# Silu by one ScalarE instruction in a selective-scan kernel, and a reordered block end

## The chip, the cores and the metric

The kernel runs on one core of a Trainium2 chip. The metric is the device time of one execution in microseconds (us). Three runs of the kernel before gave a median of 3261.13 us (3260.6 to 3262.81).

## The reference, cut to what matters

Four sequences of 1024 tokens and 512 channels go through a conditioned block with two state-space scans, one forward in time and one backward, each over 1024 inner channels and 16 states.

```python
ada = jax.nn.silu(c) @ Wada.T + bada                  # shift, scale, gate
x_ssm = _ln(_ln(x) * (1 + scale) + shift)             # skip is the inner value
mz = x_ssm @ Wz.T + bz ;  mx = x_ssm @ Wx.T + bx
act_mx = jax.nn.silu(mx)                              # what the change is about
z1 = ssm(mz @ Wc1.T + bc1) ;  z2 = flip(ssm(flip(mz @ Wc2.T + bc2)))
# inside ssm: delta = softplus(dlt @ Wdt.T + bdt), h = exp(delta*A)*h + delta*B*u, y = sum_n h*C + u*D
out = (act_mx * z1 + act_mx * z2) @ Wf.T + bf + skip
return x + gate * out
```

## The kernel before, in words

A setup part (`setup_kernel`, some 230 us) normalises the tokens, folds weights and stores intermediates. The main part (`ssm_kernel`) is one straight program of 64 units. A unit k is one tile of 128 inner channels of one direction of one sequence, all 1024 tokens: of each 16 units the first eight are the forward tiles of a sequence, the next eight its backward tiles. A unit has 16 chunks c, one for each state. In this text a unit's chunk is written as scan 0, Exp 5 and so on. Five engines run their own instruction streams in program order and meet at semaphores; SyncE (SP) issues nearly all DMAs.

For each chunk: ScalarE (ACT) computes the decay exp(delta*A) (L1218) into `dec` or into a PSUM slot; the inflow delta*B*u is made in one of three ways, by the letter of the chunk in `KINDS = "EVAVEVAPAVAPAPAV"`: E by a TensorE (PE) product with a diagonal (L939), A by ScalarE's scaling (L1159) that PE transposes (L927), V and P by GpSimd's (POOL) product in `bst` (L1257). VectorE (DVE) scans (L1352). The product with C is VectorE's for V (L1361) and GpSimd's for the others (L1262). PE transposes and sums all 16 in `y` (L916), four chunks late.

Around the scans each unit prepares the next one in the PSUM pair `mb` (1024 columns, two halves): at chunk 3 PE's product for delta (`delta_product`, L876), at chunk 4 ScalarE's `copy_y` (L1150) and `softplus_start` (Abs L1115, Exp L1117), at chunk 5 `softplus_end` (Ln, L1121) and VectorE's `finish_delta` (L1283), from chunk 7 or 9 on PE's z product (L887), VectorE's `inflow_half` (L1293) and ScalarE's `skip_half` and `copy_dut`.

The gate silu(mx) is needed once for each tile of each sequence, 32 times. It is made in the units k with k%16 from 1 to 8 (`has_mx`); these are called mx units here. Their mx product runs on PE at chunks 13 to 15 and at chunk 0 of the next unit (`mx_part`, L897). ScalarE makes the sigmoid of each half with four functions (`sigmoid_half`: Relu L1134, Exp L1137, Ln L1139, Exp L1142), half 0 at chunk 15, half 1 at chunk 1 of the next unit; VectorE's `silu_half` (L1303) multiplies each by mx + bx. The result in `silu` is stored by SP at chunk 5 and loaded again for the backward tiles.

The units k with k%16 from 9 to 15 and 0 (but not k = 0) have `gate_y` at chunk 7 (L1315) and are called gate units. From the second sequence on, a block of the output projection goes with them: PE's `project` at chunk 15 and at chunk 0 of the next unit, and VectorE's `read_projection` (L1319, four instructions) at chunk 1. `delta_product` waits for the reader of `mb` from the unit before: `silu_ready` or `proj_read`.

The tables of ScalarE: line 243 of the setup part is `nc.scalar.preload_act_table_set("natural_log_exp_and_others")`, and no other line names a table set.

Of the kernel before, what the change touches and what calls it, by code (L numbers as in the profile page):

```python
# [27 lines left out]
def setup_kernel(nc, t, scratch):  # L28

    with ExitStack() as ctx:  # L30
# [288 lines left out]
        def _(dve):  # L319
# [62 lines left out]
            nc.vector.tensor_copy(dbias[:, 1:2], ps[6][0:RD, DT * RD:DT * RD + 1]).then_inc(proj_ready[1], 1)  # L382
            dve.wait_ge(proj_ready[1], 2)
            dve.wait_ge(bcz_ready, NF)
            nc.vector.tensor_scalar(par[:, 0, :, PBX], par[:, 0, :, PBX], -LOW, None, ALU.add).then_inc(par_ready, 1)
            nc.vector.tensor_tensor(par[:, :, :, PZD], par[:, :, :, PBZ], par[:, :, :, PDP],
                                    ALU.mult).then_inc(par_ready, 1)

# [157 lines left out]
def ssm_kernel(nc, t, scratch):  # L546

    with ExitStack() as ctx:
# [3 lines left out]
        def sem(name):  # L552
            return ctx.enter_context(nc.semaphore(name))
# [29 lines left out]
            "turned", "dut_mm", "scaled", "bt_ready", "dut_ready"))  # L583
        mx_mm, ytr_mm, ud_mm, summed, proj_mm = (sem(n) for n in (
            "mx_mm", "ytr_mm", "ud_mm", "summed", "proj_mm"))
        soft_step, soft_ready, ud_ready, decay_ready, y_read, sig_step, sig_ready = (sem(n) for n in (
            "soft_step", "soft_ready", "ud_ready", "decay_ready", "y_read", "sig_step", "sig_ready"))
        delta_ready, du_ready, scanned, dve_prod, silu_ready, gated, proj_read = (sem(n) for n in (
            "delta_ready", "du_ready", "scanned", "dve_prod", "silu_ready", "gated", "proj_read"))
        pool_b, pool_prod = (sem(n) for n in ("pool_b", "pool_prod"))  # L590
# [109 lines left out]
        def _(sp):  # L700
# [68 lines left out]
            for k in range(NU):  # L769
# [3 lines left out]
                for c in range(N):  # L773
# [52 lines left out]
                        sp.wait_ge(y_read, k)  # L826
                        sp.dma_start(scratch["yf"][pair(k - 1)], yrd[:]).then_inc(y_out, 16)
                    if c == 5 and k > 0 and has_mx(k - 1) and not backward(k - 1):
                        sp.wait_ge(silu_ready, 2 * mx_index(k - 1) + 2)
                        sp.dma_start(scratch["si"][pair(k - 1)], silu[:]).then_inc(si_out, 16)  # L830
                    if c == 6 and e == ET - 2 and k + 2 < NU:
                        sp.wait_ge(dps_mm, 2 * (k + 2))
# [30 lines left out]
        def _(pe):  # L863
            def delta_product(k):
                pe.wait_ge(wdt_in[k % 2], 16 * (k // 2 + 1))
                pe.wait_ge(dl_in, 48 * (k // ET + 1))
                for h in range(2):
                    if k >= 2 and has_mx(k - 2):
                        pe.wait_ge(silu_ready, 2 * mx_index(k - 2) + h + 1)
                    elif k >= 2 and dbc_job(k - 2) is not None:  # L870
                        pe.wait_ge(dbc_ready, 2 * dbc_job(k - 2) + h + 1)
                    elif k >= 2 and h == 0 and projection_of(k - 2) is not None:
                        pe.wait_ge(proj_read, projection_of(k - 2) + 1)
                    elif k >= 1:
                        pe.wait_ge(dut_ready, 2 * k - 1 + h)
                    nc.tensor.matmul(mb[h], wdt[:, k % 2, :], dl[:, half(h)], start=True, stop=True).then_inc(dps_mm, 1)  # L876
# [230 lines left out]
        def _(act):  # L1107

            def softplus_start(k):
                if k > 0:  # L1110
                    act.wait_ge(delta_ready, k)
                if k >= 2 and has_mx(k - 2):
                    act.wait_ge(silu_ready, 2 * mx_index(k - 2) + 2)
                act.wait_ge(dps_mm, 2 * k + 2)
                nc.scalar.activation(soft[:], mbw[:], ACT.Abs).then_inc(soft_step, 1)  # L1115
                act.wait_ge(soft_step, 2 * k + 1)
                nc.scalar.activation(soft[:], soft[:], ACT.Exp, scale=-1.0).then_inc(soft_step, 1)  # L1117
# [10 lines left out]
                nc.scalar.activation(ud[:, half(h)], z_bank(k, h), ACT.Identity, scale=par[:, f // ET, f % ET, PDP:PDP + 1],  # L1128
                                     bias=par[:, f // ET, f % ET, PZD:PZD + 1]).then_inc(ud_ready, 1)

            def sigmoid_half(k, h):
                i = 2 * mx_index(k) + h
                act.wait_ge(mx_mm, i + 1)
                nc.scalar.activation(soft[:, half(h)], mb[h], ACT.Relu,  # L1134
                                     bias=par[:, 0, k % ET, PBX:PBX + 1]).then_inc(sig_step, 1)
                act.wait_ge(sig_step, 3 * i + 1)
                nc.scalar.activation(soft[:, half(h)], soft[:, half(h)], ACT.Exp, scale=-1.0).then_inc(sig_step, 1)  # L1137
                act.wait_ge(sig_step, 3 * i + 2)
                nc.scalar.activation(soft[:, half(h)], soft[:, half(h)], ACT.Ln, scale=math.exp(-LOW),  # L1139
                                     bias=1.0).then_inc(sig_step, 1)  # L1140
                act.wait_ge(sig_step, 3 * i + 3)
                nc.scalar.activation(soft[:, half(h)], soft[:, half(h)], ACT.Exp, scale=-1.0).then_inc(sig_ready, 1)  # L1142

            def copy_y(k):
                act.wait_ge(summed, N * (k + 1))
# [55 lines left out]
            for k in range(NU):  # L1201
                f, zs = wtile(k), z_step(k)
                new_b = (k + 1) % ET == 0
                for c in range(N):
                    q = N * k + c
                    if c == 0:
                        act.wait_ge(delta_ready, k + 1)
                    if kind(q) in "AE":
                        if before("AE", q) > 0:
                            act.wait_ge(scanned, TURNED[before("AE", q) - 1] + 1)  # L1210
                        decays = dec[:]
                    else:
                        if q >= 2:
                            wait_scanned_out(act, q - 2)
                        elif q == 1:
                            act.wait_ge(bt_ready, 1)
                        decays = slot[q % 2][:]
                    nc.scalar.activation(decays, delta[:, k % 2, :], ACT.Exp,  # L1218
                                         scale=par[:, f // ET, f % ET, PA + c:PA + c + 1]).then_inc(decay_ready, 1)
                    if c == LAG and k > 0:  # L1220
                        copy_y(k - 1)
                    if c == 1 and k % ET == 0:
                        make_diagonal(k // ET, 1)
                    if c in SCALE_STEPS:
                        for n, h in SCALE_STEPS[c]:
                            scale_half(N * k + n, h)
                    if c == 1 and k > 0 and has_mx(k - 1):
                        sigmoid_half(k - 1, 1)
                    if c in (0, 1) and k > 0 and dbc_job(k - 1) is not None:
                        evict_dbc(dbc_job(k - 1), c)  # L1230
                    if k + 1 < NU:
                        if c == 4:
                            softplus_start(k + 1)
                        if c == 5:
                            softplus_end(k + 1)
                        if c in (zs + 2, zs + 4):
                            skip_half(k + 1, (c - zs - 2) // 2)
                        if c == zs + 4 and new_b:
                            copy_bt((k + 1) // ET)
                        if c == 14 and new_b:  # L1240
                            make_diagonal((k + 1) // ET, 0)
                        if c == zs + 5:
                            copy_dut(k + 1, 0)
                        if c == min(zs + 7, N - 1):
                            copy_dut(k + 1, 1)
                    if c == 15 and has_mx(k):
                        sigmoid_half(k, 0)
            copy_y(NU - 1)

        @block.gpsimd  # L1250
# [27 lines left out]
        def _(dve):  # L1278
# [15 lines left out]
                                               scalar=par[:, f // ET, f % ET, PBZ:PBZ + 1],  # L1294
                                               in1=delta[:, k % 2, half(h)], op0=ALU.add, op1=ALU.mult).then_inc(du_ready, 1)

            def silu_half(k, h):
                dve.wait_ge(sig_ready, 2 * mx_index(k) + h + 1)
                if h == 0:
                    stored = k // (2 * ET) * (ET - 1) + (ET - 1 if backward(k) else k % ET - 1)  # L1300
                    if stored > 0:
                        dve.wait_ge(si_out, 16 * stored)
                nc.vector.scalar_tensor_tensor(out=silu[:, half(h)], in0=mb[h],  # L1303
                                               scalar=par[:, 1, k % ET, PBX:PBX + 1],
                                               in1=soft[:, half(h)], op0=ALU.add, op1=ALU.mult).then_inc(silu_ready, 1)

            def gate_y(k):
                b, e = k // (2 * ET), k % ET
                if e > 0:
                    dve.wait_ge(si_in, 16 * ((ET - 1) * b + e))  # L1310
                else:
                    dve.wait_ge(silu_ready, 2 * mx_index(k) + 2)
                bank = mbw if k < NU - 1 else slot[0]
                dve.wait_ge(ytr_mm, 2 * pair(k) + 2)
                nc.vector.tensor_tensor(ybuf[:], bank[:], silu[:], ALU.mult).then_inc(gated, 1)  # L1315
# [21 lines left out]
            for k in range(NU):  # L1337
                zs = z_step(k)
                step = -1 if backward(k) else 1
                for c in range(N):  # L1340
# [8 lines left out]
                    if q >= HR:  # L1349
# [1 line left out]
                    h = slot[q % 2] if kind(q) == "V" else hbuf[:, q % HR, :]  # L1351
                    nc.vector.tensor_tensor_scan(h[:, ::step], decays[:, ::step], inflows[:, ::step], 0.0,  # L1352
                                                 ALU.mult, ALU.add).then_inc(scanned, 1)
                    if c == 1 and k > 0 and projection_of(k - 1) is not None:
                        read_projection(projection_of(k - 1), mb[0])
                    if c == 5 and k + 1 < NU:
                        finish_delta(k + 1)
                    if kind(q) == "V":
# [1 line left out]
                        dve.wait_ge(c_in[c], 16 * (q // SEQ + 1))  # L1360
                        nc.vector.tensor_tensor(hbuf[:, q % HR, :], slot[q % 2][:], cres[:, c, :],  # L1361
                                                ALU.mult).then_inc(dve_prod, 1)
                    if c == 1 and k > 0:
                        if has_mx(k - 1):
                            silu_half(k - 1, 1)
                    if c == 5 and k == NU - 1:
                        read_projection(projection_of(k), mb[1])
                    if c == 7 and gates(k):
                        gate_y(k - 1)
                    if c in (zs + 2, zs + 4) and k + 1 < NU:  # L1370
                        inflow_half(k + 1, (c - zs - 2) // 2)
                    if c == 15 and has_mx(k):
                        silu_half(k, 0)
            gate_y(NU - 1)
            dve.wait_ge(rest_in, 32 * ET)
            for i in range(TAIL, B * ET):
# [78 lines left out]
```

## Time and profile before

| what | value |
| --- | --- |
| median of 3 runs | 3261.13 us |
| profiled execution, its own time | 3260.72 us |
| its span, first to last instruction | 3258.9 us |
| mean granted TensorE clock | 0.987 |
| units 0 to 63, first scan to last scan | 234.1 to 3198.9 us |

All durations below are from this one profiled execution; 1.8 us of its time lie around its span. A timeline row reads: start in us, duration in us, engine, line, operation, output<-input, shapes, number of merged instructions, and in brackets the idle time of the engine before it with what ended it. Successive instructions of an engine overlap a little, so that a start can lie some 0.1 us before the end of the one before.

### The profile page before, as it was taken

What the parts mean: (1) busy time and instruction counts of PE and PEld (TensorE: products, weight loads), DVE (VectorE), ACT (ScalarE), POOL (GpSimd) and SP (SyncE); (2) the same over time, 40 slices, a digit from 0 to 9 for tenths busy, and PEclk for the clock granted to TensorE, in tenths of its full rate; (3) what the DMA queues carried; (4) which work ended last, traced back from release to release, by engine and by line L of the source; (5) the groups of instructions that cost most, each with busy time, mean ns of one, the idle gap of its engine ahead of it and who ended that gap; (6) DMA issues with size and microseconds to landing.
All of it is one profiled execution on the core that took longest, in us unless ns stands there. A gap on an engine that the chain in (4) does not pass through costs nothing.

```text
span 3258.9 us, 54891 instructions
## 1 busy us (share of the span) xinstructions
PE 2982.0 (92%) x19924; PEld 2368.9 (73%) x19924; DVE 3015.8 (93%) x2008; ACT 2676.7 (82%) x5150; POOL 2901.4 (89%) x1280
## 2 busy tenths in 40 slices
PE   8979999999999999999989999899999999899999
PEld 5866666666767667678877666678777666677789
DVE  2839999999999999999999999999999999999994
ACT  1548999988888999987788999987878999988772
POOL 0539999999999999999999999999999999999993
PEclk9989999999999999999999999999999999999999
DMA  5774334645474343644574334645566333645463
GB/s 223 276 241 176 127 131 141 211 164 175 159 279 161 127 134 132 221 153 147 167 263 169 131 121 135 224 140 167 167 218 215 118 134 131 227 141 166 154 201 109
DMA packets 207197, 560.40 MB, mean 172 GB/s; under 512 B 20216, under 2 KB 66744, under 8 KB 202704
## 3 DMA queue, kind: packets, MB, share of 16 engines
q1 hardware_dynamic: 203568, 538.01, 49.6%
q10 hardware_dynamic: 2208, 10.49, 0.9%
q0 software_dynamic: 1152, 8.39, 0.7%
q8 instruction: 159, 2.61, 0.3%
q14 instruction: 110, 0.90, 0.1%
HBM read 476.19 MB, written 80.63 MB: 171 GB/s over the span
## 4 chain that ended last, share of the span: by engine, by line
PE 50%; ACT 21%; DVE 12%; issue 10%; DVEq 0%; ACTq 0%
PE y L916 14%; PE slot L927 10%; PE mb L887 9%; ACT abuf L1159 8%; PE mb L1000 6%; DVE hbuf L1352 6%; ACT slot L1218 3%; DVE hbuf L1361 3%; PE mb L897 3%; PE slot L939 3%; DVE slot L1352 3%; ACT dec L1218 2%; ACT soft L1115 2%; PE mb L958 2%; PE mb L993 1%
## 5 line engine op out<-in xcount | busy, mean ns | idle before, releaser
L1262 POOL TENSOR_TENSOR hbuf<-hbuf,cres 128x1024 f32<-128x1024 f32 x704 | 1665.5, 2380 | 138.1 <-DVE hbuf L1352 137.9
L1257 POOL TENSOR_TENSOR bst<-bst,du 128x1024 f32<-128x1024 f32 x512 | 1224.6, 2392 | 33.5 <-DVE du L1293 33.5
L1352 DVE TENSOR_TENSOR_SCAN hbuf<-dec,slot 128x1024 f32<-128x1024 f32 x512 | 1165.0, 2275 | 35.6 <-PE slot L939 28.4
L916 PE MATMUL y<-ident,hbuf 128*128 128x128 f32 x8192 | 1016.2, 273 | 0.1
L916 PEld LDWEIGHTS y<-ident,hbuf 128*128 128x128 f32 x8192 | 924.2, 141 | 104.6 <-issue 104.0
L1159 ACT ACTIVATE abuf<-dut,bt 128x128 f32<-128x128 f32 x3072 | 964.7, 387 | 0.0
L1352 DVE TENSOR_TENSOR_SCAN slot<-slot,bst 128x1024 f32<-128x1024 f32 x320 | 728.2, 2276 | 21.1 <-ACT slot L1218 21.0
L1218 ACT ACTIVATE slot<-delta,par 128x1024 f32<-128x1024 f32 x512 | 568.2, 1110 | 196.4 <-DVE hbuf L1361 183.4
L1218 ACT ACTIVATE dec<-delta,par 128x1024 f32<-128x1024 f32 x512 | 584.1, 1141 | 113.8 <-DVE hbuf L1352 113.2
L927 PE MATMUL slot<-ident,abuf 128*128 128x128 f32 x3072 | 409.2, 276 | 168.2 <-ACT abuf L1159 157.4
L927 PEld LDWEIGHTS slot<-ident,abuf 128*128 128x128 f32 x3072 | 339.5, 141 | 301.0 <-ACT abuf L1159 240.2
L887 PE MATMUL mb<-xn,wzs 128*128 128x512 f32 x1008 | 478.9, 597 | 14.8 <-DVE ybuf L1315 11.7
L1352 DVE TENSOR_TENSOR_SCAN hbuf<-slot,bst 128x1024 f32<-128x1024 f32 x192 | 434.7, 2264 | 0.1
L1361 DVE TENSOR_TENSOR hbuf<-slot,cres 128x1024 f32<-128x1024 f32 x320 | 390.7, 1221 | 8.0
L939 PEld LDWEIGHTS slot<-diag,dut 128*128 128x128 f32 x2048 | 261.3, 203 | 103.8 <-issue 100.2
L939 PE MATMUL slot<-diag,dut 128*128 128x128 f32 x2048 | 270.2, 289 | 40.7 <-DVE hbuf L1352 37.7
L887 PEld LDWEIGHTS mb<-xn,wzs 128*128 128x128 f32 x1008 | 171.6, 190 | 145.8 <-issue 143.6
L897 PE MATMUL mb<-xn,wx 128*128 128x512 f32 x512 | 240.9, 593 | 0.0
L1000 PE MATMUL mb<-ybuf,wf 128*128 128x128 f32 x1504 | 176.4, 275 | 3.6 <-issue 3.6
L1000 PEld LDWEIGHTS mb<-ybuf,wf 128*128 128x128 f32 x1504 | 171.9, 192 | 4.0 <-issue 4.0
L876 PE MATMUL mb<-dl,wdt 81*128 81x512 f32 x252 | 130.9, 622 | 11.9 <-DVE silu L1303 10.0
L897 PEld LDWEIGHTS mb<-xn,wx 128*128 128x128 f32 x512 | 87.3, 190 | 61.2 <-issue 61.2
(170 smaller groups left out, 2283.9 us busy)
## 6 DMA issues: line engine op xcount, KB each, us to landing
bst<-bc_s SPq DMA_DIRECT2D x512, 512.0 KB, 4.0
cres<-bc_s SPq DMA_DIRECT2D x128, 512.0 KB, 7.0
wzs<-wz_s SPq DMA_DIRECT2D x64, 256.0 KB, 4.2
yf_s<-yrd SPq DMA_DIRECT2D x32, 512.0 KB, 5.4
ybuf<-yf_s SPq DMA_DIRECT2D x32, 512.0 KB, 5.0
yg_s<-ybuf SPq DMA_DIRECT2D x31, 512.0 KB, 4.4
si_s<-silu SPq DMA_DIRECT2D x28, 512.0 KB, 6.1
silu<-si_s SPq DMA_DIRECT2D x28, 512.0 KB, 5.4
```

Source lines behind the costliest of these rows:

```text
L887: last = nc.tensor.matmul(z_bank(k, h), wz[:, i * P:(i + 1) * P], xn[:, h, i, :], start=(i == 0), stop=(i == DT - 1))
L897: last = nc.tensor.matmul(mb[h], wx[:, i * P:(i + 1) * P], xn[:, h, i, :], start=(i == 0), stop=(i == DT - 1))
L916: last = nc.tensor.matmul(y[:, j * P:(j + 1) * P], hbuf[:, q % HR, j * P:(j + 1) * P], ident[:], start=False, stop=(q % N == N - 1), is_tr ...
L927: last = nc.tensor.matmul(slot[q % 2][:, j * P:(j + 1) * P], abuf[:, a % 2, j * P:(j + 1) * P], ident[:], start=True, stop=True, is_transp ...
L939: last = nc.tensor.matmul(slot[q % 2][:, j * P:(j + 1) * P], dut[:, j * P:(j + 1) * P], diag[:, i, j, :], start=True, stop=True)
L1000: nc.tensor.matmul(bank[:, m * P:(m + 1) * P], wf[:, e, m * P:(m + 1) * P], tokens, start=(e == 0 and m == 0), stop=False, skip_group_chec ...
L1159: last = nc.scalar.activation(abuf[:, a % 2, j * P:(j + 1) * P], dut[:, j * P:(j + 1) * P], ACT.Copy, scale=bt[:, g % 2, j, n:n + 1])
L1218: nc.scalar.activation(decays, delta[:, k % 2, :], ACT.Exp, scale=par[:, f // ET, f % ET, PA + c:PA + c + 1]).then_inc(decay_ready, 1)
L1257: nc.gpsimd.tensor_tensor(bst[:, i % BR, :], bst[:, i % BR, :], du[:, k % 2, :], ALU.mult).then_inc(pool_b, 1)
L1262: nc.gpsimd.tensor_tensor(hbuf[:, q % HR, :], hbuf[:, q % HR, :], cres[:, q % N, :], ALU.mult).then_inc(pool_prod, 1)
L1352: nc.vector.tensor_tensor_scan(h[:, ::step], decays[:, ::step], inflows[:, ::step], 0.0, ALU.mult, ALU.add).then_inc(scanned, 1)
L1361: nc.vector.tensor_tensor(hbuf[:, q % HR, :], slot[q % 2][:], cres[:, c, :], ALU.mult).then_inc(dve_prod, 1)
```

## The change

ScalarE computes Silu with its own function, over both halves at once, with the bias bx, and writes `silu` directly. It is issued at chunk 1 of the next unit, where half 1 was. The four functions for each half and VectorE's two products go; so do the additions of 40 to bx. What waited for a half of silu waits for the whole; ScalarE now waits for the store of `silu` (`si_out`), which VectorE did. In VectorE's stream `read_projection` at chunk 1 comes behind that chunk's product with C, where it was ahead of it.

```diff
-            nc.vector.tensor_scalar(par[:, 0, :, PBX], par[:, 0, :, PBX], -LOW, None, ALU.add).then_inc(par_ready, 1)
...
-                        sp.wait_ge(silu_ready, 2 * mx_index(k - 1) + 2)
+                        sp.wait_ge(silu_ready, mx_index(k - 1) + 1)
                         sp.dma_start(scratch["si"][pair(k - 1)], silu[:]).then_inc(si_out, 16)
...
                     if k >= 2 and has_mx(k - 2):
-                        pe.wait_ge(silu_ready, 2 * mx_index(k - 2) + h + 1)
+                        pe.wait_ge(silu_ready, mx_index(k - 2) + 1)
...
-                if k >= 2 and has_mx(k - 2):
-                    act.wait_ge(silu_ready, 2 * mx_index(k - 2) + 2)
                 act.wait_ge(dps_mm, 2 * k + 2)
...
-            def sigmoid_half(k, h):
...
+            def make_silu(k):
+                act.wait_ge(mx_mm, 2 * mx_index(k) + 2)
+                if mx_index(k) > 0:
+                    stored = k // (2 * ET) * (ET - 1) + (ET - 1 if backward(k) else k % ET - 1)
+                    act.wait_ge(si_out, 16 * stored)
+                nc.scalar.activation(silu[:], mbw[:], ACT.Silu, bias=par[:, 0, k % ET, PBX:PBX + 1]).then_inc(silu_ready, 1)
...
                     if c == 1 and k > 0 and has_mx(k - 1):
-                        sigmoid_half(k - 1, 1)
+                        make_silu(k - 1)
...
-                    if c == 15 and has_mx(k):
-                        sigmoid_half(k, 0)
...
-            def silu_half(k, h):
...
                     nc.vector.tensor_tensor_scan(h[:, ::step], decays[:, ::step], inflows[:, ::step], 0.0,
                                                  ALU.mult, ALU.add).then_inc(scanned, 1)
-                    if c == 1 and k > 0 and projection_of(k - 1) is not None:
-                        read_projection(projection_of(k - 1), mb[0])
...
                         nc.vector.tensor_tensor(hbuf[:, q % HR, :], slot[q % 2][:], cres[:, c, :],
                                                 ALU.mult).then_inc(dve_prod, 1)
-                    if c == 1 and k > 0:
-                        if has_mx(k - 1):
-                            silu_half(k - 1, 1)
+                    if c == 1 and k > 0 and projection_of(k - 1) is not None:
+                        read_projection(projection_of(k - 1), mb[0])
...
-                    if c == 15 and has_mx(k):
-                        silu_half(k, 0)
```

## Rows read from the trace of the kernel before

**Rows 1.** The page, part 1: busy time, share and instructions of each engine.

```profile
PE 2982.0 (92%) x19924; PEld 2368.9 (73%) x19924; DVE 3015.8 (93%) x2008; ACT 2676.7 (82%) x5150; POOL 2901.4 (89%) x1280
```

**Rows 2.** Instruction groups: count, busy us, mean ns, idle before with releaser.

```profile
L1303 DVE SCALAR_TENSOR_TENSOR silu<-mb,par,soft 128x512 f32<-128x512 f32 x64 | 47.5, 743 | 5.5 <-ACT soft L1142 5.5
L1134 ACT ACTIVATE soft<-mb,par 128x512 f32<-128x512 f32 x64 | 43.3, 677 | 20.1 <-PE mb L897 20.1
...
L1142 ACT ACTIVATE soft<-soft 128x512 f32<-128x512 f32 x64 | 40.4, 631 | 2.0
...
L1319 DVE SCALAR_TENSOR_TENSOR xres<-mb,gate_sb,xres 128x128 f32<-128x128 f32 x92 | 25.9, 345 | 8.1 <-PE mb L1005 8.1
...
L243 ACT ACT_TABLE_LOAD x1 | 1.3, 1283 | 1.8 <-issue 1.8
```

**Rows 3.** Timeline of VectorE, unit 4 up to unit 5's first scan.

```profile
415.05 2.29 DVE L1352 TENSOR_TENSOR_SCAN hbuf<-dec,slot 128x1024 f32<-128x1024 f32 x1
417.71 2.30 DVE L1352 TENSOR_TENSOR_SCAN slot<-slot,bst 128x1024 f32<-128x1024 f32 x1 [0.38 <-ACT slot L1218]
...
421.85 2.27 DVE L1352 TENSOR_TENSOR_SCAN hbuf<-dec,slot 128x1024 f32<-128x1024 f32 x1
...
431.86 1.21 DVE L1283 SCALAR_TENSOR_TENSOR delta<-mb,soft 128x1024 f32<-128x1024 f32 x1
...
434.11 2.28 DVE L1352 TENSOR_TENSOR_SCAN hbuf<-dec,slot 128x1024 f32<-128x1024 f32 x1
...
459.79 0.74 DVE L1303 SCALAR_TENSOR_TENSOR silu<-mb,par,soft 128x512 f32<-128x512 f32 x1
460.55 2.29 DVE L1352 TENSOR_TENSOR_SCAN hbuf<-dec,slot 128x1024 f32<-128x1024 f32 x1
```

**Rows 4.** Timeline of ScalarE, the same unit.

```profile
416.58 1.10 ACT L1218 ACTIVATE slot<-delta,par 128x1024 f32<-128x1024 f32 x1
417.62 0.67 ACT L1134 ACTIVATE soft<-mb,par 128x512 f32<-128x512 f32 x1
...
430.33 1.04 ACT L1121 ACTIVATE soft<-soft 128x1024 f32<-128x1024 f32 x1
431.28 1.13 ACT L1218 ACTIVATE dec<-delta,par 128x1024 f32<-128x1024 f32 x1
...
434.23 1.12 ACT L1218 ACTIVATE slot<-delta,par 128x1024 f32<-128x1024 f32 x1 [0.65 <-DVE hbuf L1361]
435.28 1.26 ACT L1159 ACTIVATE abuf<-dut,bt 128x128 f32<-128x128 f32 x4
```

**Rows 5.** Timeline of TensorE, the same unit.

```profile
415.67 1.88 PE L897 MATMUL mb<-xn,wx 128*128 128x512 f32 x4
...
436.60 1.09 PE L927 MATMUL slot<-ident,abuf 128*128 128x128 f32 x8 [1.43 <-ACT abuf L1159]
...
458.51 1.95 PE L939 MATMUL slot<-diag,dut 128*128 128x128 f32 x16
```

**Rows 6.** Timeline of GpSimd, the same unit.

```profile
436.53 4.68 POOL L1262 TENSOR_TENSOR hbuf<-hbuf,cres 128x1024 f32<-128x1024 f32 x2 [1.26 <-DVE hbuf L1352]
```

**Rows 7.** Timeline of VectorE, a gate unit with projection (unit 29).

```profile
1574.79 1.13 DVE L1319 SCALAR_TENSOR_TENSOR xres<-mb,gate_sb,xres 128x128 f32<-128x128 f32 x4 [0.35 <-PE mb L1005]
...
1589.23 2.27 DVE L1352 TENSOR_TENSOR_SCAN hbuf<-dec,slot 128x1024 f32<-128x1024 f32 x1
```

**Rows 8.** Timeline of ScalarE, the same gate unit, Exp 6.

```profile
1586.41 1.14 ACT L1218 ACTIVATE dec<-delta,par 128x1024 f32<-128x1024 f32 x1
```

**Rows 9.** Timeline of TensorE, the same gate unit, chunk 10's transposes.

```profile
1597.14 1.06 PE L927 MATMUL slot<-ident,abuf 128*128 128x128 f32 x8 [0.24 <-DVE hbuf L1352]
```

**Rows 10.** Timeline of TensorE, unit 8, chunks 3 and 4.

```profile
607.51 2.08 PE L876 MATMUL mb<-dl,wdt 81*128 81x512 f32 x2 [2.50 <-DVE silu L1303]
610.17 3.72 PE L939 MATMUL slot<-diag,dut 128*128 128x128 f32 x16 [0.59 <-DVE hbuf L1352]
```

**Rows 11.** Busy us of each engine, granted clock, DMA share, GB/s there.

```profile
606.00:612.00 6.00, 3.90 (x10) 2.36 (x11) 5.01 (x3) 5.82 (x10) 3.93 (x2) 0.58 0.75 263
```

More of the change, by code:

```diff
@@ L585, in ssm_kernel @@
             "mx_mm", "ytr_mm", "ud_mm", "summed", "proj_mm"))
-        soft_step, soft_ready, ud_ready, decay_ready, y_read, sig_step, sig_ready = (sem(n) for n in (
-            "soft_step", "soft_ready", "ud_ready", "decay_ready", "y_read", "sig_step", "sig_ready"))
+        soft_step, soft_ready, ud_ready, decay_ready, y_read = (sem(n) for n in (
+            "soft_step", "soft_ready", "ud_ready", "decay_ready", "y_read"))
         delta_ready, du_ready, scanned, dve_prod, silu_ready, gated, proj_read = (sem(n) for n in (
@@ L1129, in skip_half @@
                                      bias=par[:, f // ET, f % ET, PZD:PZD + 1]).then_inc(ud_ready, 1)
-            def sigmoid_half(k, h):
[L1132 to L1142, printed above, removed]
+            def make_silu(k):
[4 more added lines that the diff above has]
+                nc.scalar.activation(silu[:], mbw[:], ACT.Silu, bias=par[:, 0, k % ET, PBX:PBX + 1]).then_inc(silu_ready, 1)
             def copy_y(k):
@@ L1295, in inflow_half @@
                                                in1=delta[:, k % 2, half(h)], op0=ALU.add, op1=ALU.mult).then_inc(du_ready, 1)
-            def silu_half(k, h):
[L1298 to L1305, printed above, removed]
             def gate_y(k):
@@ L1311, in gate_y @@
                 else:
-                    dve.wait_ge(silu_ready, 2 * mx_index(k) + 2)
+                    dve.wait_ge(silu_ready, mx_index(k) + 1)
                 bank = mbw if k < NU - 1 else slot[0]
```

## The prediction

> **What bounds the kernel now.** I read the page's busy shares first: VectorE 93%, TensorE 92%, GpSimd 89%, ScalarE 82% [rows 1]. Four engines near full mean that the shares decide nothing, so I went to the timelines of a whole unit. The mx units repeat almost exactly: unit 4's first scan starts at 415.05 and unit 5's at 460.55, a period of 45.50 us [rows 3]. What closes this cycle? TensorE starts chunk 8's transposes at 436.60, after 1.43 us of idle time that ScalarE's `abuf` ended, and its timeline then has no gap until the spread product for the next scan 0, which ends at 458.51 + 1.95 = 460.46 [rows 5]. Scan 0 starts 0.09 us behind it, although the silu product ahead of it ended at 460.53 and other successors start before the end of the one before [rows 3]. So TensorE's block of 23.9 us is one leg. Before it: ScalarE's Exp 7 at 434.23, which had waited 0.65 us for VectorE's product 5, then the scaling at 435.28, which ends at 436.54 [rows 4]. Ahead of that lies VectorE, nearly without idle time, from scan 0 on. The cycle is thus VectorE from scan 0 to product 5, two ScalarE instructions, TensorE to the next scan 0. GpSimd is not on it, with 1.26 us idle in a unit [rows 6], but it would cap a gain at that.
>
> **The change, part by part.**
>
> *VectorE's silu products.* Sixty-four of 0.743 us, 47.5 us [rows 2]. Half 0 stands ahead of scan 0, where TensorE sets the start: its removal gives nothing by itself, since the cover is TensorE's block. Half 1 stands between scan 1 and scan 2, on the path.
>
> *ScalarE's eight functions a tile.* 43.3 + 3 x 40.4 = 164.5 us in all [rows 2]. Gone from chunk 15, they let Exp 0, the scalings and Exp 1 run earlier, and the 0.38 us that scan 1 waited for Exp 1 goes [rows 3]. So without ScalarE, scan 2 could come 0.38 + 0.66 = 1.04 us earlier than its 6.80 us behind scan 0.
>
> *The new Silu with its tables.* Silu brings its table load and a second load when Exp comes back. The one load in this trace takes 1.283 us [rows 2]; the nearest bounds are that row alone, and twice it, if the engine must stop and refill as long as it loads. Successive instructions of ScalarE start 0.06 to 0.09 us ahead of the end of the one before [rows 4], which a load would break; I take 1.4 us a load, near the lower bound, since those rows show an engine that hardly pauses between instructions. The first load needs no data; I let it run ahead of the wait for mx, where it is covered. Silu itself starts when the mx product ends, 415.67 + 1.88 = 417.55, or 2.5 us behind scan 0 [rows 5], and costs as much as a 1024-wide Exp with a pointer operand, 1.10 us [rows 4]. Then load 1.3, Exp 2 1.14 with small steps between: scan 2 at 2.57 + 1.11 + 1.35 + 1.19 = 6.22 us instead of 6.80. That is -0.57 us, in 32 units: **-18 us**. Were the first load behind the wait for mx, it would be +0.8, thus +26 in place of -18.
>
> *Which table comes back.* This is what I think decides. Softplus uses Exp and then Ln in every unit, and with one load in the whole execution [rows 2] they share a table now, the one that line 243 names. Nothing in the change names a table behind Silu. That line 243 had to name its set speaks for an Exp by itself finding another one, without Ln. If so, from unit 2 on every Ln at chunk 5 needs a load, and Exp 6 behind it another: 61 units with two loads more, 122 in all, with the 64 of Silu 186. The Trainium skill, "ScalarE: Activation LUTs", in "Table sets: the hidden batching unit", says that Exp's common set lacks Ln, and that one named set holds both. No row here shows that.
>
> The price of these two in an mx unit: Ln starts at 430.33, so Exp 6 at 431.28 is late by 2.8 [rows 4]; the scaling of chunk 8's first half follows and Exp 7 starts at about 436.3 instead of 434.23, since its 0.65 us of idle time absorb the rest. The scaling and TensorE's block are late by **2.06 us**. VectorE is late by less: finish_delta (431.86 [rows 3]) waits for Ln and scan 6 for Exp 6, some 1.2 us. The units: 31 (the 32 mx units but unit 1): **+64 us**.
>
> In a gate unit Exp 6 starts at 1586.41 [rows 8]; 2.8 later it ends at 1590.35, and scan 6, now at 1589.23 [rows 7], is late by **1.17 us**. Exp 7 and the rest follow with idle time in hand. From there VectorE runs without pause to scan 8, and TensorE waits for that at 1597.14 [rows 9], so this passes on to the next scan 0. Gate units with k from 9 to 62: 30, **+35 us**.
>
> *read_projection behind product 1.* It waited 0.35 us for TensorE [rows 7], 8.1 us in 23 (92 instructions, 4 each) [rows 2]. Behind the product of 1.2 us this is covered: **-8 us**. The delta product waits for the read, which ends no later than the two together ended before.
>
> *SP, GpSimd and the setup.* No DMA is added or moved; the store of silu is issued at chunk 5 as before, and Silu ends earlier than half 1's product did. The wait for `si_out` moves from VectorE to ScalarE, and that store is a whole unit old. The dropped addition in the setup is one small instruction. Zero for all.
>
> *TensorE's clock.* Where TensorE idled 2.50 and then 0.59 us in unit 8, the granted clock of 606 to 612 us was 0.58, thus part at 1.2 GHz, and the spread product took 3.72 us instead of 1.95 [rows 5, 10, 11]. Late scalings leave it idle for 1.43 + 2.06 = 3.5 us ahead of its block in 31 mx units, interrupted by one product. The price is 0 to 1.77 us a unit, 0 to 55 us; I take two in three, **+37 us**. In gate units I count nothing, since the block starts some microseconds behind the gap.
>
> **The sum** on the profiled execution's own time: 3260.7 - 18 + 64 + 35 - 8 + 37 = 3371 us. The median shown is 0.4 us above this execution, so nothing is to be corrected. 0.2% (6.5 us) is about what a measurement of this kernel can tell from no change.
>
> **A rule against it.** The Trainium skill, same page, in "What ACT_TABLE_LOAD costs", gives each switch a drain beside the load and 2.66 us in all. By that price the sum would be near the first rival's.
>
> **The rivals.**
>
> 1. *A load stops the engine for about its own length again.* The mechanism: nothing overlaps a load, so the 122 loads on the path and the 32 ahead of Exp 2 cost 1.28 more each, +197: 3568 us. For it: only one load is in the trace, with an idle engine around it, so its surroundings are unseen. Against it: the overlap of 0.06 to 0.09 us between ScalarE's instructions [rows 4]. Half of that would give about 3470.
>
> 2. *Exp's load brings the table back that has Ln too* (faster). Then only 64 loads are there, the first of each pair covered by the wait for mx, the second reaching scan 2 before 6.80 us. It decides as long as Silu's way from mx to Exp 2's end takes under 4.2 us. -18 - 8: 3235 us. For it: one named table demonstrably serves both. Against it: nothing in the program names it again.
>
> 3. *The change doesn't bring loads at all*, because Silu shares the table. Then scan 2 gains 1.03 us in 32 units, GpSimd's cap of 1.26 not reached: -33 - 8: 3220 us. The description speaks against it.
>
> 4. *The 186 loads come, but find ScalarE idle*, as 18% of its time is [rows 1]. Then only a few microseconds are left, the result within 0.2%. Against: the idle time of 0.65 us [rows 4] is what is there at this place.
>
> **How the numbers follow.** The forecast has 0.74, rival 1 0.16 (0.08 of it near its full price), rival 2 0.06, rival 3 0.02, rival 4 0.02. The forecast's own ends: without clock loss 3334, and with somewhat more cover 3305; with a clock loss in every unit and some in gate units 3410. The range goes on to 3475, half of rival 1, and leaves out its full price and the faster cases: 3305 to 3475. Faster by over 0.2%: 0.08; within: 0.02; slower: 0.90.
>
> **What would show it.** Some 186 further ACT_TABLE_LOAD rows, at Silu, Exp 2, Ln and Exp 6, near 1.28 us each; Silu one row of 1.1 us; mx period about 47 to 48 us, with TensorE idle 3 us or more ahead of chunk 8's transposes; scan 2 at 6.2 behind scan 0; finish_delta waiting for Ln; the 8.1 us of L1319 gone; the clock mean below 0.987. It is wrong if Ln has no load, or if a gap near 1.3 us stands beside each load.

## The result, and the profile after

The changed kernel takes 3368.09 us (median of 4 runs, 3364.08 to 3373.39), the kernel before 3261.97 in the same comparison: a ratio of 1.0324, 95% interval 1.0311 to 1.0336. The forecast was 3371 us, in a range of 3305 to 3475. The profiled execution has a span of 3366.4 us and a mean granted TensorE clock of 0.979, where before it was 0.987.

Part 1 of the page of the changed kernel, beside [rows 1]:

```profile
PE 3001.3 (89%) x19924; PEld 2405.4 (71%) x19924; DVE 2994.6 (89%) x1943; ACT 2802.1 (83%) x5112; POOL 2900.3 (86%) x1280
```

VectorE's busy time fell by 21 us and its share by four points. The durations of its instructions, added up, fell by 43.5 us, nearly the 47.5 of [rows 2]; the page counts the overlap of two neighbours once, and with the products gone and new waits between neighbours less of it is left. ScalarE's busy time rose by 125 us although it has 38 instructions fewer. The instruction groups of the changed kernel (columns as in [rows 2]) say with what:

```profile
L1209 ACT ACT_TABLE_LOAD x93 | 119.3, 1283 | 1.7
...
L1118 ACT ACT_TABLE_LOAD x61 | 78.3, 1283 | 1.1
...
L1133 ACT ACT_TABLE_LOAD x32 | 41.1, 1283 | 0.6
...
L1133 ACT ACTIVATE silu<-mb,par 128x1024 f32<-128x1024 f32 x32 | 35.8, 1118 | 36.4 <-PE mb L896 36.4
L1298 DVE SCALAR_TENSOR_TENSOR xres<-mb,gate_sb,xres 128x128 f32<-128x128 f32 x92 | 25.7, 342 | 0.0
```

In the changed file L1133 is Silu, L1118 is Ln and L1209 the decays' Exp. There are 32 loads at Silu, 61 at Ln and 93 = 32 + 61 at the Exp behind either: the 186 of the forecast, each 1.283 us. The last row is `read_projection`: its 8.1 us of waiting [rows 2] are gone.

ScalarE's timeline in unit 4 of the changed kernel, beside [rows 4]:

```profile
416.20 1.11 ACT L1209 ACTIVATE slot<-delta,par 128x1024 f32<-128x1024 f32 x1
417.33 1.28 ACT L1133 ACT_TABLE_LOAD   x1
419.93 1.12 ACT L1133 ACTIVATE silu<-mb,par 128x1024 f32<-128x1024 f32 x1 [1.32 <-PE mb L896]
421.07 1.28 ACT L1209 ACT_TABLE_LOAD   x1
422.36 1.15 ACT L1209 ACTIVATE dec<-delta,par 128x1024 f32<-128x1024 f32 x1
...
430.88 1.26 ACT L1150 ACTIVATE abuf<-dut,bt 128x128 f32<-128x128 f32 x4
432.16 1.28 ACT L1118 ACT_TABLE_LOAD   x1
433.45 1.06 ACT L1118 ACTIVATE soft<-soft 128x1024 f32<-128x1024 f32 x1
434.53 1.28 ACT L1209 ACT_TABLE_LOAD   x1
435.82 1.15 ACT L1209 ACTIVATE dec<-delta,par 128x1024 f32<-128x1024 f32 x1
```

Two readings. The first load stands ahead of Silu's wait: it ends at 418.61 and ScalarE then waits 1.32 us for the mx product, so this load is covered. And a load leaves gaps of only 0.01 to 0.02 us around it (433.45 + 1.06 = 434.51, load at 434.53, ending at 435.81, Exp 6 at 435.82). What it costs is its duration and the overlap of some 0.1 us that two neighbours lose: 1.4 us.

VectorE's timeline in the same unit, beside [rows 3]:

```profile
417.39 2.29 DVE L1331 TENSOR_TENSOR_SCAN hbuf<-dec,slot 128x1024 f32<-128x1024 f32 x1 [1.24 <-ACT slot L1209]
...
423.54 2.29 DVE L1331 TENSOR_TENSOR_SCAN hbuf<-dec,slot 128x1024 f32<-128x1024 f32 x1 [0.41 <-ACT dec L1209]
...
434.54 1.23 DVE L1272 SCALAR_TENSOR_TENSOR delta<-mb,soft 128x1024 f32<-128x1024 f32 x1 [0.88 <-ACT soft L1118]
...
437.01 2.29 DVE L1331 TENSOR_TENSOR_SCAN hbuf<-dec,slot 128x1024 f32<-128x1024 f32 x1
```

Scan 2 comes 6.15 us behind scan 0, where it was 6.80. Then finish_delta waits for Ln, and scan 6 starts 13.47 us behind scan 2 instead of 12.26. The first row puts scan 0's wait down to Exp 1, which ended at 417.31. The spread product ended at 417.30 (the first row below), and with one table scan 0 starts before Exp 1 has ended (rows of the first run), so that TensorE released it here, too.

TensorE's timeline, the spread product for unit 4's scan 0 and then around chunk 8's transposes, in unit 4 and in unit 5, beside [rows 5]:

```profile
415.35 1.95 PE L938 MATMUL slot<-diag,dut 128*128 128x128 f32 x16
...
435.92 1.95 PE L886 MATMUL mb<-xn,wzs 128*128 128x512 f32 x4 [0.88 <-DVE delta L1272]
...
440.40 1.97 PE L926 MATMUL slot<-ident,abuf 128*128 128x128 f32 x8 [2.53 <-ACT abuf L1150]
...
488.72 1.09 PE L926 MATMUL slot<-ident,abuf 128*128 128x128 f32 x8 [2.53 <-ACT abuf L1150]
```

Four microseconds from these transposes on, in unit 4 and in unit 5, as windows (length, busy us of PE, PEld, DVE, ACT and POOL, granted clock, DMA share, GB/s):

```profile
440.00:444.00 4.00, 3.60 (x17) 3.42 (x18) 3.01 (x2) 4.00 (x10) 4.00 (x2) 0.58 0.34 112
...
488.00:492.00 4.00, 3.28 (x20) 2.52 (x21) 3.89 (x2) 4.00 (x10) 4.00 (x2) 1.00 0.23 89
```

Both units idle 0.88 and 2.53 us there. In unit 4 the clock is partly at 1.2 GHz behind that (0.58), and eight transposes take 1.97 us; in unit 5 it stays at 2.4 GHz and they take 1.09. Unit 4's period is 48.32 us, unit 5's 46.90. From scan 0 to the transposes both take 23.01 us, where it was 21.55; from there to the next scan 0 unit 5 takes 23.89, as before (23.95), and unit 4 25.31. Of the 20 plain mx units (k%16 from 2 to 6) 12 are long ones. Why of two units with the same idle time one loses the clock and the other doesn't, no run shows.

### The profile page after: what moved, and what is told of

Read it like the earlier page. It is cut to its first block, busy times and chain, and to the rows that moved or that the text cites. A ratio compares the mean times of both kernels' runs of the same rounds, so it can differ in the third digit from the quotient of the medians.

```text
span 3366.4 us, 54788 instructions
## 1 busy us (share of the span) xinstructions
PE 3001.3 (89%) x19924; PEld 2405.4 (71%) x19924; DVE 2994.6 (89%) x1943; ACT 2802.1 (83%) x5112; POOL 2900.3 (86%) x1280
## 4 chain that ended last, share of the span: by engine, by line
PE 56%; ACT 29%; issue 5%; DVE 4%; ACTq 0%; DVEq 0%
PE y L915 17%; PE mb L886 10%; PE slot L926 8%; ACT abuf L1150 7%; PE mb L999 6%; PE mb L896 6%; ACT slot L1209 4%; ACT L1209 4%; ACT dec L1209 4%; PE slot L938 3%; DVE hbuf L1331 3%; ACT L1118 2%; ACT soft L1118 2%; ACT soft L1112 2%; ACT yrd L1141 2%
## 5 line engine op out<-in xcount | busy, mean ns | idle before, releaser
L915 PE MATMUL y<-ident,hbuf 128*128 128x128 f32 x8192 | 1038.2, 276 | 0.0
L915 PEld LDWEIGHTS y<-ident,hbuf 128*128 128x128 f32 x8192 | 948.6, 144 | 104.0 <-issue 104.0
L1209 ACT ACTIVATE dec<-delta,par 128x1024 f32<-128x1024 f32 x512 | 586.2, 1145 | 127.9 <-DVE hbuf L1331 120.8
L1209 ACT ACTIVATE slot<-delta,par 128x1024 f32<-128x1024 f32 x512 | 565.9, 1105 | 100.3 <-DVE hbuf L1338 98.5
L926 PE MATMUL slot<-ident,abuf 128*128 128x128 f32 x3072 | 429.2, 285 | 229.0 <-ACT abuf L1150 224.2
L926 PEld LDWEIGHTS slot<-ident,abuf 128*128 128x128 f32 x3072 | 357.1, 146 | 356.6 <-ACT abuf L1150 317.6
L938 PEld LDWEIGHTS slot<-diag,dut 128*128 128x128 f32 x2048 | 251.4, 197 | 102.5 <-issue 98.9
L938 PE MATMUL slot<-diag,dut 128*128 128x128 f32 x2048 | 260.0, 282 | 41.3 <-DVE hbuf L1331 38.3
L1272 DVE SCALAR_TENSOR_TENSOR delta<-mb,soft 128x1024 f32<-128x1024 f32 x64 | 78.3, 1224 | 67.9 <-ACT soft L1118 67.9
```

The costliest lines, as they stand in the source:

```text
L915: last = nc.tensor.matmul(y[:, j * P:(j + 1) * P], hbuf[:, q % HR, j * P:(j + 1) * P], ident[:], start=False, stop=(q % N == N - 1), is_tr ...
L926: last = nc.tensor.matmul(slot[q % 2][:, j * P:(j + 1) * P], abuf[:, a % 2, j * P:(j + 1) * P], ident[:], start=True, stop=True, is_transp ...
L938: last = nc.tensor.matmul(slot[q % 2][:, j * P:(j + 1) * P], dut[:, j * P:(j + 1) * P], diag[:, i, j, :], start=True, stop=True)
L1209: nc.scalar.activation(decays, delta[:, k % 2, :], ACT.Exp, scale=par[:, f // ET, f % ET, PA + c:PA + c + 1]).then_inc(decay_ready, 1)
```

## The experiments

Times are compared through the ratio to the kernel before, which ran beside each (3265.5 us in the first four, 3266.1 in the next four, 3264.7 in the last two).

**One table for Exp and Ln.**

```diff
                 nc.scalar.activation(silu[:], mbw[:], ACT.Silu, ...).then_inc(silu_ready, 1)
+                nc.scalar.preload_act_table_set("natural_log_exp_and_others")
```

> The changed kernel with one more line: right behind Silu ScalarE loads the table set that line 243 names, which holds both Exp and Ln. 64 loads more than before instead of 186. Theory (the cost lies in the loads at Ln and Exp 6): mx period near 44.9 us, gate units with projection near 46.4, total 3235 us (3228 to 3242), faster than the kernel before by 0.8%. Rival (Silu's own two loads, or Silu itself, carry the loss): the time stays above 3300 us. Second rival (VectorE was the bound, its 1.4 us a unit come off): near 3212 us.

3235.33 us, ratio 0.9903 (0.9888 to 0.9918). Plain mx units take 44.88 us, gate units with projection 46.40. Naming the table in this one place takes off the whole 3.2% and 1% more, as the theory said; both rivals, above 3300 and 3212 us, are out. So the loss lay in the loads at Ln and Exp 6 and in what follows from them, and neither in Silu nor in its own two loads. Its unit 4, ScalarE and VectorE's scan 0:

```profile
414.18 1.10 ACT L1210 ACTIVATE slot<-delta,par 128x1024 f32<-128x1024 f32 x1
415.30 1.28 ACT L1133 ACT_TABLE_LOAD   x1
417.36 1.12 ACT L1133 ACTIVATE silu<-mb,par 128x1024 f32<-128x1024 f32 x1 [0.77 <-PE mb L896]
418.49 1.28 ACT L1134 ACT_TABLE_LOAD   x1
419.79 1.15 ACT L1210 ACTIVATE dec<-delta,par 128x1024 f32<-128x1024 f32 x1
...
414.82 2.29 DVE L1332 TENSOR_TENSOR_SCAN hbuf<-dec,slot 128x1024 f32<-128x1024 f32 x1 [0.69 <-PE slot L938]
```

VectorE waits 0.69 us for the spread product ahead of scan 0. That is the room in which silu half 0 stood.

**The order of read_projection alone,** in the kernel before.

```diff
-                    if c == 1 and k > 0 and projection_of(k - 1) is not None:
-                        read_projection(projection_of(k - 1), mb[0])
                     if c == 5 and k + 1 < NU:
...
+                    if c == 1 and k > 0 and projection_of(k - 1) is not None:
+                        read_projection(projection_of(k - 1), mb[0])
                     if c == 1 and k > 0:
```

> The kernel before with read_projection behind product 1 as the only edit. Theory: the wait of 0.35 us for TensorE is covered in 23 units: 3254.5 us (3253 to 3257), a ratio of 0.9977. Rival (TensorE's or ScalarE's streams set scan 2 there, or the delta product now waits for the read): no difference.

3258.24 us, ratio 0.9978 (0.9968 to 0.9987), some 7 us: the ratio is the expected one, and the time is higher because the kernel before took 3265.5 us beside it. Gate units with projection go from 46.72 to 46.41 us. VectorE there, beside [rows 7], no longer waits:

```profile
1573.16 1.23 DVE L1359 TENSOR_TENSOR hbuf<-slot,cres 128x1024 f32<-128x1024 f32 x1
1574.31 1.12 DVE L1319 SCALAR_TENSOR_TENSOR xres<-mb,gate_sb,xres 128x128 f32<-128x128 f32 x4
```

**The 122 loads alone,** in the kernel before.

```diff
+                if k > 2:
+                    nc.scalar.preload_act_table_set("natural_log")
                 nc.scalar.activation(soft[:], soft[:], ACT.Ln, bias=1.0).then_inc(soft_ready, 1)
+                if k > 2:
+                    nc.scalar.preload_act_table_set("natural_log_exp_and_others")
```

 Theory: the loads alone carry the loss, some 2.0 us in 31 mx units, 1.2 us in 30 gate units, and some 35 us of low TensorE clock: 3392 us (3365 to 3405), more than the changed kernel. Rival (the loss needs the later Silu): under 3320 us.

3380.75 us, ratio 1.0345 (1.033 to 1.0359). Its plain mx units take 47.57 us (median; +2.07), its gate units with projection 47.95 (+1.23): the forecast's two prices, 2.06 and 1.17. The loss without any Silu shows that the loads are enough to cause it. Silu and the new order take 24 us off between the profiled executions of the kernel before and of that with one table (unit 0 to unit 63), but the changed kernel is only 7 us faster than this one by the ratios, 12 by the profiled executions. In the plain mx units their gain, 20 x 0.62 = 12 us, is lost again: 12 of the 20 are long in the changed kernel and 4 in this one, each by some 1.5 us.

```profile
433.78 1.28 ACT L1121 ACT_TABLE_LOAD   x1
435.08 1.06 ACT L1123 ACTIVATE soft<-soft 128x1024 f32<-128x1024 f32 x1
436.15 1.28 ACT L1125 ACT_TABLE_LOAD   x1
437.45 1.15 ACT L1222 ACTIVATE dec<-delta,par 128x1024 f32<-128x1024 f32 x1
```

**TensorE kept busy,** in the changed kernel.

```diff
+                if h == 0 and 0 in ks and k > 0 and not gates(k - 1):
+                    for i in range(2):
+                        nc.tensor.matmul(z_bank(k, h), wz[:, i * P:(i + 1) * P], xn[:, h, i, :], start=True, stop=True)
                 for i in ks:
```

> The changed kernel, with TensorE given two superfluous matmuls of 128x512 ahead of the z product at chunk 7 of the non-gate units (their result is overwritten by the real product). They fill 1.7 us of the 2.5 us that it idles ahead of chunk 8's transposes. Theory (about half of the mx units lose 1.6 us to TensorE's clock at 1.2 GHz behind that gap): the units of 48.3 to 48.6 us fall to 46.9, total near 3342 us (3335 to 3352). Rival (the longer units have another cause, or the extra work costs as much as it saves): 3365 us or more.

3343.68 us, ratio 1.0236 (1.0222 to 1.025), against 1.0324 for the changed kernel: more work on TensorE and 0.9% less time. All 20 plain mx units now take 46.92 to 46.94 us. Its unit 4: the idle time ahead of chunk 8 is 0.83 us, and the window behind it has full clock.

```profile
434.82 1.96 PE L887 MATMUL mb<-xn,wzs 128*128 128x512 f32 x4 [0.88 <-DVE delta L1275]
436.61 1.88 PE L889 MATMUL mb<-xn,wzs 128*128 128x512 f32 x4
439.32 1.09 PE L929 MATMUL slot<-ident,abuf 128*128 128x128 f32 x8 [0.83 <-ACT abuf L1153]
```

```profile
440.00:444.00 4.00, 4.00 (x25) 2.90 (x24) 3.88 (x3) 4.00 (x11) 4.00 (x3) 1.00 0.35 131
```

The six runs that follow all start from the kernel with one table.

**The old read order with it.** The edit of the second run, backwards.

```diff
+                    if c == 1 and k > 0 and projection_of(k - 1) is not None:
+                        read_projection(projection_of(k - 1), mb[0])
                     if c == 5 and k + 1 < NU:
...
-                    if c == 1 and k > 0 and projection_of(k - 1) is not None:
-                        read_projection(projection_of(k - 1), mb[0])
```

> The kernel with one table named behind Silu, and read_projection back ahead of product 1. Theory (Silu and the order are two separate gains): 7.5 us more than with the new order, 3243 us where the kernel before has 3262, ratio 0.9940. Rival (with Silu in, the order no longer counts): ratio 0.990 as with the new order.

3240.61 us, ratio 0.9924 (0.9911 to 0.9936). That lies between the two expectations, 0.9940 and 0.990, with both outside its interval, and the interval overlaps the one with the new order (0.9888 to 0.9918), so that the ratio alone doesn't decide. The unit periods do: gate units with projection take 46.72 again, against 46.40, and plain mx units 44.86, nearly unchanged. The fifteen such units with k%16 from 10 to 14 make 15 x 0.32 = 4.8 us. So the gains are separate, and the order's is somewhat smaller than the 7.5 us expected.

**A third load behind Silu.**

```diff
                 nc.scalar.activation(silu[:], mbw[:], ACT.Silu, ...).then_inc(silu_ready, 1)
+                nc.scalar.preload_act_table_set("exp_and_others")
                 nc.scalar.preload_act_table_set("natural_log_exp_and_others")
```

> The kernel with one table named behind Silu, and a third load of another set between Silu and that load, 32 more, all ahead of Exp 2. Theory (a load costs its 1.28 us and next to nothing around it, and lies on the path here): scan 2 at 7.43 us behind scan 0 instead of 6.15, each of 32 units longer by 1.28, in all +41 us, 3276 us, ratio 1.004. Rival (a load stops the engine for about its own length again): +82 us. Second rival (it finds ScalarE idle): no difference from the kernel with one table.

3282.09 us, ratio 1.0054 (1.0039 to 1.0069), some 49 us more than with one table by the ratios and 41 between the two profiled executions. Scan 2 stands at 7.44 us instead of 6.15, one load (1.29 us) later, and plain mx units take 46.14 at the least (+1.26) and 46.31 in the median. What goes beyond 41 us is not taken apart; the mean granted clock of 0.982 against 0.991 fits a further clock loss. The rival with a stop of a load's own length is out:

```profile
420.18 1.28 ACT L1134 ACT_TABLE_LOAD   x1
421.47 1.28 ACT L1135 ACT_TABLE_LOAD   x1
422.76 1.15 ACT L1211 ACTIVATE dec<-delta,par 128x1024 f32<-128x1024 f32 x1
```

**A third load ahead of Silu.**

```diff
             def make_silu(k):
+                nc.scalar.preload_act_table_set("natural_log_exp_and_others")
```

> The kernel with one table named behind Silu, and an extra load ahead of Silu's own, 32 more, where ScalarE waits for the mx product anyway (1.32 us in unit 4 of the changed kernel). Theory: covered, no difference from the kernel with one table, 3235 to 3240 us, ratio 0.991. Rival (each load costs wherever it stands): +41 us.

3256.67 us, ratio 0.9972 (0.9963 to 0.9981): both expectations missed, some 22 us more by the ratios instead of 0 or 41.

```profile
415.24 1.28 ACT L1129 ACT_TABLE_LOAD   x1
416.52 1.28 ACT L1134 ACT_TABLE_LOAD   x1
417.82 1.11 ACT L1134 ACTIVATE silu<-mb,par 128x1024 f32<-128x1024 f32 x1
```

My mistake was the cover. I took 1.32 us from the changed kernel, where TensorE's late block gives ScalarE a lead; in this base it is 0.77 (the first run's rows). 1.28 - 0.77 = 0.51 us stick out, and the plain mx units are longer by 0.53 (45.41 against 44.88). For the four units with k%16 = 8, whose Silu doesn't wait, scan 2 is a whole load later (9.82 against 8.54). 28 x 0.53 + 4 x 1.28 = 20 us, nearly what was measured.

**Padding on VectorE.**

```diff
+                    if c == 15 and has_mx(k) and k > 1:
+                        dve.wait_ge(si_out, 16 * (k // (2 * ET) * (ET - 1) + (ET - 1 if backward(k) else k % ET - 1)))
+                        nc.vector.scalar_tensor_tensor(out=silu[:, half(0)], in0=silu[:, half(0)], scalar=1.0,
+                                                       in1=silu[:, half(0)], op0=ALU.min, op1=ALU.min).then_inc(pad_done, 1)
...
+                    act.wait_ge(pad_done, mx_index(k))
```

> The kernel with one table named behind Silu, and on VectorE in 31 mx units a superfluous product-like instruction of 128x512 at chunk 15, where silu half 0 stood (it leaves its values unchanged). Theory (TensorE's block sets scan 0, half 0 was covered): at most 5 us more than with one table, 3235 to 3240 us. Rival (VectorE is the bound): +23 us, 3258 us.

3398.16 us, ratio 1.0414 (1.0393 to 1.0436): some 165 us more than with one table, far outside both. The instruction meant to take 0.74 us took 7.5. VectorE, and GpSimd in the same stretch:

```profile
418.07 7.54 DVE L1344 SCALAR_TENSOR_TENSOR silu<-silu 128x512 f32<-128x512 f32 x1
425.54 2.27 DVE L1333 TENSOR_TENSOR_SCAN hbuf<-dec,slot 128x1024 f32<-128x1024 f32 x1
```

```profile
418.07 2.39 POOL L1248 TENSOR_TENSOR bst<-bst,du 128x1024 f32<-128x1024 f32 x1
420.38 2.38 POOL L1253 TENSOR_TENSOR hbuf<-hbuf,cres 128x1024 f32<-128x1024 f32 x1
422.69 2.37 POOL L1248 TENSOR_TENSOR bst<-bst,du 128x1024 f32<-128x1024 f32 x1
427.95 2.35 POOL L1253 TENSOR_TENSOR hbuf<-hbuf,cres 128x1024 f32<-128x1024 f32 x1 [2.89 <-DVE hbuf L1333]
```

GpSimd ran three instructions back to back and ended at 425.06; VectorE's ended 0.55 us later. At the end of unit 5 VectorE's took 2.90 us, and GpSimd's instruction that began beside it took 2.79:

```profile
520.14 2.90 DVE L1344 SCALAR_TENSOR_TENSOR silu<-silu 128x512 f32<-128x512 f32 x1
...
522.46 2.79 POOL L1253 TENSOR_TENSOR hbuf<-hbuf,cres 128x1024 f32<-128x1024 f32 x1
```

The run thus says nothing on its question, and the next one asks it with other operands.

**The same padding with one operand in PSUM,** those of the old silu half 0. The instruction below takes the place of the padding above; the rest stays.

```diff
+                        dve.wait_ge(mx_mm, 2 * mx_index(k) + 1)
+                        nc.vector.scalar_tensor_tensor(out=silu[:, half(0)], in0=mb[0], scalar=par[:, 1, k % ET, PBX:PBX + 1],
+                                                       in1=silu[:, half(0)], op0=ALU.add, op1=ALU.mult).then_inc(pad_done, 1)
```

> As the padding run, but the superfluous VectorE instruction at chunk 15 of 31 mx units has the operands of the old silu half 0: the mx product's half 0 in PSUM and one SBUF operand. (The values that it leaves are overwritten by Silu.) Theory (the 7.5 us of the padding came from its two SBUF operands beside GpSimd's instructions; half 0 itself lay under TensorE's block): the instruction takes 0.74 us, the total is that with one table or up to 5 us more, ratio to the kernel before 0.990 to 0.992. Rival (VectorE's load decides, however it is read): 7 us each again, 3390 us. Second rival (half 0 was on the path): +23 us, ratio 0.998.

3232.38 us, ratio 0.9904 (0.9888 to 0.9921): no difference from the kernel with one table. 31 instructions of 0.74 us, 23 us of VectorE's time, cost nothing where TensorE sets scan 0: plain mx units take 44.86 us. They fill the 0.69 us that VectorE waited there almost exactly, so that a longer instruction is not tested. In the four units with k%16 = 7 the same instruction does cost nearly its length: 46.59 us against 45.96. The four behind them are shorter by 0.7 to 1.9, which hides it in the total.

```profile
410.67 0.74 DVE L1345 SCALAR_TENSOR_TENSOR silu<-mb,par,silu 128x512 f32<-128x512 f32 x1
411.43 2.29 DVE L1333 TENSOR_TENSOR_SCAN hbuf<-dec,slot 128x1024 f32<-128x1024 f32 x1
```

```profile
409.39 1.95 PE L938 MATMUL slot<-diag,dut 128*128 128x128 f32 x16
```

The spread product ends at 411.34, after which scan 0 starts 0.09 us later, as in [rows 3, 5].

**The second diagonal later,** the version that came out fastest.

```diff
-                    if c == 1 and k % ET == 0:
+                    if c == (2 if k > 0 and has_mx(k - 1) else 1) and k % ET == 0:
                         make_diagonal(k // ET, 1)
```

(The two lines also moved behind `make_silu`.)

> The kernel with one table named behind Silu, and in the four mx units that begin a direction (k%16 = 8) the second diagonal of chunk 4 is made at chunk 2 instead of chunk 1, behind Silu and Exp 2. Theory: there scan 2 comes 2.4 us earlier (6.15 instead of 8.54 behind scan 0), scan 3 loses 1.3 of it, and TensorE idles less: 4 to 10 us less in all, 3229 us, ratio 0.988. Rival (Exp 3 or the spread product for chunk 4 then comes too late): 3235 us or more.

3228.81 us, ratio 0.9889 (0.9874 to 0.9904). Unit 8 falls from 48.72 to 46.81 us, with scan 2 at 6.17 instead of 8.54. The unit shows it; the whole-kernel ratio overlaps that of the kernel with one table, so that a gain of some 5 us over it (4.6 by the ratios, 6.5 by the medians) is likely and not proved by the totals.

## Why the prediction was right

The mechanism, the 186 loads and the prices in the plain units came out as worked out. That the total came within 3 us is in part luck. Between the profiled executions the mx units (k%16 from 1 to 8) grew by 65 us, where -18 + 64 + 37 = 83 was forecast, and the gate units by 44, where 35 - 8 = 27 was. The two errors, 18 and 17 us, nearly cancelled.

- *What bounds the kernel.* Right. The cycle VectorE, ScalarE, TensorE's block to scan 0 was shown by the VectorE padding that cost nothing and by the loads at Ln, whose full lateness reached the next scan 0 through TensorE.
- *Silu's half 0 and ScalarE's chunk 15 give nothing, half 1 something.* Right in the plain mx units: scan 2 came 0.65 us earlier (0.57 forecast), and such a unit with one table is 0.62 shorter. Wrong in the four units with k%16 = 7, where half 0 was on the path: by the padding it cost 0.63 us each.
- *The first load of a pair is covered.* Right for the forecast's kernel, with 1.32 us to spare. The cover is smaller, 0.77 us, once the loads at Ln are gone.
- *A load costs 1.4 us.* Right. The Trainium skill, "ScalarE: Activation LUTs", in "What ACT_TABLE_LOAD costs", gives 1283 ns for the load, which this trace confirms, and a drain of 1380 ns with every switch, which it doesn't: the gaps are 0.02 us, and a further load moved scan 2 by 1.29. The measurement decides; the first rival falls.
- *The table that comes back lacks Ln.* The loads at 61 Ln and 61 Exp 6 show it, and naming the set removed them. The same page's table of sets agrees: the only set that it lists with Ln is the one that line 243 names.
- *+64 in mx units, +35 in gate units.* 2.07 and 1.23 us a unit in the median with the loads alone, against 2.06 and 1.17.
- *read_projection, -8.* -7 alone.
- *TensorE's clock, +37.* The size was near and the place partly wrong. I gave it to mx units in two of three; 12 of 20 plain ones are long, and keeping TensorE busy there took back 24 us by the medians, 29 by the ratios. But I counted nothing in gate units, and there 3 of 15 with projection and 4 of 5 of the first sequence (units 10 to 14) are longer than the shortest of their kind by 1.2 to 1.6 us, with a granted clock of 0.96 or 0.97 over the unit where the short ones have 1.00.
- *The units with k%16 = 7 and 8.* I treated them as the others. Those with 7 went from 47.22 to 48.03 us only. Those with 8 went from 48.15 to 50.93: Silu and its loads stand there behind a diagonal of 2.4 us, and scan 2 comes only 0.3 us earlier (8.53 against 8.82 behind scan 0). What makes up the rest of the 2.8 us is not taken apart.
- *The second rival* was the right account of another kernel: with the table named behind Silu the time is 3235 us, the number it gave. The match is closer than the account: the kernel before took 3265.5 us beside it, so that the saving is 32 us (27 to 37 by the interval) where it gave 26.

## What to carry to other kernels

When a function with its own table enters a stream, count the switches for every later function, too: with the two loads at the new function alone the kernel is 1% faster than before, while the 122 that its return left at an untouched Exp and Ln cost 4%. Loads at the new function aren't free by themselves: a third one ahead of it, where ScalarE mostly waits, cost 22 us, and behind it 49. Name the wanted set behind that function, and check it in the profile by the count of load rows and their lines. Before filling or freeing an engine, ask which engine ends last at that place: 23 us of extra VectorE work cost nothing, and 1.7 us of extra TensorE work in each mx unit of the changed kernel took 0.9% off.

## What the runs showed that was not expected

VectorE's `scalar_tensor_tensor` of 128x512 with both inputs in SBUF took 7.5 us in the median beside GpSimd's unbroken stream (1.08 to 7.8 us over 31 of them), and 0.74 us with one input in PSUM in the same place. In all 31 it ended 0.5 to 0.6 us behind the end of one of GpSimd's instructions. In 27 that was the last before GpSimd itself had to wait for VectorE's scan. In the other four, 1.08 to 2.96 us long, GpSimd's stream went on, and its next instruction took 2.8 us instead of 2.37. So VectorE's instruction could get in between two of GpSimd's, and mostly didn't.

The Trainium skill, "GPSIMD Engine Reference", in "Specifications", says that GpSimd shares its SBUF interfaces with VectorE and that the two contend when VectorE's instruction has two SBUF inputs; these rows agree. The setup part of the kernel before is no test of it: the same kind with two SBUF inputs (L364) takes 0.74 us there, but apart from the first 0.06 us only GpSimd's 128x4 products and its DMA issues run beside it. That the time is contention is read from where the instructions end and was not tested further: the two padding runs differ in the function, too, and the first had one tensor as both inputs and output.
